# A recommender tower kernel: first-layer chunks spread over four tiles, and known parts of the MLP moved into the last quad

## The chip, the core and the metric

The kernel runs on one core of a Trainium2 chip. The metric is the device time of one execution, in microseconds (us). It is launched once, with all inputs in device memory.

## What is computed

The reference looks up 39 embedding rows of 16 floats for each of 512 samples, runs three layers of a compressed interaction network over them, and feeds the summed layers and a dense context to a small MLP. Everything is float32.

```python
def cin_layer(X0, Xi, W, b):                   # W: (128, 39 * Fi)
    return einsum('hjk,bjd,bkd->bhd', W.reshape(128, 39, Fi), X0, Xi) + b
e = stack([tbl_f[ids[:, f]] for f in range(39)], axis=1)     # 512 x 39 x 16
X1 = cin_layer(e, e, W0, b0); X2 = cin_layer(e, X1, W1, b1); X3 = cin_layer(e, X2, W2, b2)
z = concat([X1.sum(2), X2.sum(2), X3.sum(2), dense_ctx])     # 128 + 128 + 128 + 16
h = relu(z @ W_top1 + b_top1)                                # 400 -> 512
h = relu(h @ W_top2 + b_top2)                                # 512 -> 256
y = h @ W_top3                                               # 256 -> 1
```

## The kernel before, in words

**Tiles and quads.** A tile T is 8 samples times 16 dimensions = 128 columns; there are 64. Four tiles are a quad q (512 columns); there are 16. `ti` is a tile's place in its quad, 0 to 3. In the last quad there is no next quad to prepare.

**Layer 1, the main loop.** `layer1(T, g)` (L645) multiplies a tile of X1 with W1 in ten groups g of up to four fields, by three matmuls of 512 columns (L657 to L659: high and low parts). Their results go round a ring of five PSUM banks, `ps_y`, so group g needs the bank that group g-5 has left (for g below 5: group g+5 of the tile before). Seven groups (0, 1, 3, 4, 6, 7, 9) are scaled by ACT (`scale`, L415), three (2, 5, 8) by DVE (`scale_and_sum`, L527 and L529), into `prod`. POOL adds two pairs of ACT's groups (`add_groups`, L323): the first when ACT has done group 1, the second when ACT has done group 4. DVE reduces the early half (`reduce_early`, L536) after POOL's second add, then scales group 8, then reduces the late half (`reduce_late`, L544). ACT may begin the next tile only when the early half is reduced. `sum_d` (L665) multiplies the reduced tile with a block pattern, and ACT keeps the result (`keep_g`, L424).

**Layer 0, one quad ahead.** While quad q runs its tiles, X1 of quad q+1 is made. SP copies three blocks of rows (`share_rows`, L237, three DMAs) and cuts six windows (`cut_window`, L242, six DMAs) as soon as the rows are there. POOL multiplies each of seven chunks c = 0 to 6 with the shared rows (`multiply`, L318) and signals `z_made`. TensorE then runs `layer0(q+1, c)` (L600), one fp32 matmul, which shows as two instructions, into the bank `ps_x1`.

**The order of the work** is written out by hand. POOL runs, for each tile, the first add, `between(q, ti, 0)`, the second add, `between(q, ti, 1)`. `MULTIPLIED_IN` (L66) says in which of these places chunks are multiplied, and `GATHERED_IN` (L67) where the table rows of quad q+3 are gathered (L298, ten per quad). `SUMMED_AFTER` (L69) says after which (ti, group) TensorE runs each layer-0 chunk. TensorE executes its list in order and waits where an operand is not ready.

**The end.** After the last tile TensorE makes the MLP's first layer in four banks of `ps_y` from four inputs: the dense context (16 rows) and X1's sums `r1` (both known early), X2's sums (after the last `sum_d`) and X3's sums `r3`. `r3` comes from 39 fp32 matmuls (L703, 78 instructions) over all samples. Then come the second layer (L713) and the third (L718). The bias is added to `r1` by DVE after the last tile (L570).

Of the kernel before, what the change touches and what calls it, by code (L numbers as in the profile page):

```python
# [5 lines left out]
ALU = mybir.AluOpType  # L6
ACT = mybir.ActivationFunctionType
# [18 lines left out]
SPC = 3  # L26
CHUNKS = -(-SHIFTS // SPC)
REP = SPC * F
MOVES = SPC + CHUNKS - 1
XROWS = REP + CHUNKS - 1  # L30
FPG = P // QB
GATHERS = -(-F // FPG)
# [30 lines left out]
REDUCTIONS = 2  # L63


MULTIPLIED_IN = {(1, 0): range(0, 1), (1, 1): range(1, 4), (2, 0): range(4, 5), (2, 1): range(5, CHUNKS)}  # L66
GATHERED_IN = {(0, 0): range(0, 1), (0, 1): range(1, 5), (3, 0): range(5, 6), (3, 1): range(6, GATHERS)}  # L67
REPEATED_IN = (2, 1)
SUMMED_AFTER = {(1, 8): 0, (2, 0): 1, (2, 2): 2, (2, 4): 3, (2, 6): 4, (2, 9): 5, (3, 1): 6}  # L69
SUM_D_AFTER = 6  # L70


HALF = FIRST[GROUPS // 2] * H
# [36 lines left out]
def build(nc, dense_ctx, ids, bases, table, W_top1, b_top1, W_top2, b_top2, W_top3, W0, b0, W1, b1, W2, b2, out):  # L110
# [8 lines left out]
    with ExitStack() as ctx:  # L119
# [3 lines left out]
        def sem(name):  # L123
            return ctx.enter_context(nc.semaphore(name))
# [73 lines left out]
        shifted = [sem("shifted_0"), sem("shifted_1")]  # L198
# [19 lines left out]
        def _(sp):  # L218
# [46 lines left out]
            sp.dma_start(dense_t_dram, dense_out).then_inc(w2_saved, 16)  # L265
            for q in range(1, QUADS):
                sp.wait_ge(x0_made, q + 1)
                share_rows(q, shifted[q % 2])
                for c in range(1, CHUNKS):
                    cut_window(q, c, shifted[q % 2])  # L270
                if q + 1 < QUADS:
                    lay_out(q + 1)

# [15 lines left out]
        def _(pool):  # L289
# [20 lines left out]

            def multiply(q, c):
                if c == 0:
                    wait(pool, shifted[q % 2], 16 * MOVES * ((q + 1) // 2))
                r = chunk_rows(c)
                window = bz[0:r, c, :] if c else x0[0:r, q % 2, :]
                if c == 0:
                    wait(pool, z_used, CHUNKS * (q - 1) + 1)
# [40 lines left out]
        def _(act):  # L358
# [94 lines left out]
            nc.scalar.copy(y_row[0:1, :], ps_tr[0:1, :]).then_inc(y_out, 1)  # L453

        @block.vector
        def _(dve):
# [94 lines left out]
            for T in range(TILES):  # L551
                q, ti = T // QT, T % QT
                if ti == 0:
                    dve.wait_ge(xt_made, q + 1)
                if T > 0:
                    reduce_late(T - 1)
                scale_and_sum(T, DVE_GROUPS[0])
                scale_and_sum(T, DVE_GROUPS[1])
                if ti == 3 and q + 1 < QUADS:
                    split_x1(q + 1)  # L560
                reduce_early(T)
                scale_and_sum(T, DVE_GROUPS[2])
                if ti == 3 and q + 1 < QUADS:
                    sum_x1(q + 1)
                if ti == 1 and q + 1 < QUADS:
                    spread(q + 1)
            reduce_late(TILES - 1)
            dve.wait_ge(bsum_made, 1)
            dve.wait_ge(r1_made, QUADS)
            nc.vector.tensor_scalar(r1[:], r1[:], b02_sum[:, 0:1], None, ALU.add).then_inc(r1_done, 1)  # L570

        @block.tensor
        def _(pe):
# [71 lines left out]
            def layer1(T, g):  # L645
# [12 lines left out]
                nc.tensor.matmul(y, hi, w1_lo[:, cols], start=False, stop=False)  # L658
                nc.tensor.matmul(y, lo, w1_hi[:, cols], start=False, stop=True).then_inc(y_made, 1)  # L659

            def sum_d(T):
                pe.wait_ge(reduced, REDUCTIONS * (T + 1))
                pe.wait_ge(bd_made, T // QT + 1)
                wait(pe, g_kept, T)
                nc.tensor.matmul(ps_g[:, 0:(F + 1) * TB], x2[:, T % 2, :],  # L665
                                 bd[:, T // QT % 2, T % QT].rearrange("p j b -> p (j b)"),
                                 start=True, stop=True).then_inc(g_summed, 1)

            for T in range(TILES):
# [4 lines left out]
                for g in range(GROUPS):  # L674
# [10 lines left out]
            def mlp1(c, rows_c, z, start, stop):  # L685
                for m in range(MC1):
                    ins = nc.tensor.matmul(ps_y[:, m, :], wt1[0:rows_c, c, m * P:(m + 1) * P], z,  # L687
                                           start=start, stop=stop)
                    if stop:
                        ins.then_inc(h1_summed, 1)  # L690
# [17 lines left out]
            for m in range(MC2):  # L708
                dst = ps_y[:, YBANKS - 1, :] if m == 0 else ps_g[:]
                for c in range(MC1):  # L710
                    if m == 0:
                        pe.wait_ge(h1_made, c + 1)
                    ins = nc.tensor.matmul(dst, wt2[:, c, m * P:(m + 1) * P], h1[:, c, :],  # L713
                                           start=c == 0, stop=c == MC1 - 1)
                ins.then_inc(h2_summed, 1)
# [39 lines left out]
```

## Time and profile before

| | before |
|---|---|
| median of three runs | 722.71 us (721.22 to 723.44) |
| the profiled execution | 718.87 us |
| its span, first to last instruction | 717.1 us |
| TensorE busy | 671.6 us, 94% |
| ScalarE (ACT) busy | 541.1 us, 75% |
| VectorE (DVE) busy | 469.7 us, 66% |
| GpSimd (POOL) busy | 460.5 us, 64% |
| mean granted TensorE clock | 0.983 of full speed |

Times in a timeline are a start and a length in us from the span's first instruction, then engine, line, operation, output and inputs, and in brackets the idle time of that engine just before it with what released it. Matmul ends are modelled, so two matmuls in a row overlap on paper. The reliable number is the distance from start to start. A table of stretches gives, for each stretch, its length, the busy time (and number of instructions) of PE, PEld (weight load), DVE, ACT and POOL, the granted clock, the busy share of the DMA engines, and GB/s.

### The profile page before, as it was taken

Reading aid. Unit: us, or ns where it says so; the run is one execution under the profiler, and the core shown is the slowest. Engines: PE = TensorE matmul, PEld = TensorE weight load, DVE = VectorE, ACT = ScalarE, POOL = GpSimd, SP = SyncE. Lnnn points to the kernel's source line nnn. Section 1 sums busy time; section 2 is a strip of 40 time slices with the busy share of each in tenths; the row PEclk is TensorE's granted clock in tenths of the full one; section 3 lists DMA queues with packets and bytes.
Section 4 is the critical chain, followed back from the end, with each engine's and each line's share of the span. In section 5 each row is a group of like instructions: output and inputs, shape, how many; then the busy total and the mean of one; then the engine's idle time right before and its main releaser. Section 6 shows DMA issues by size and latency. Waiting matters only on the chain. (4 is left out here: it accounts for less than half of the span.)

```text
span 717.1 us, 10090 instructions
## 1 busy us (share of the span) xinstructions
PE 671.6 (94%) x2631; PEld 481.9 (67%) x2631; DVE 469.7 (66%) x954; ACT 541.1 (75%) x1939; POOL 460.5 (64%) x445
## 2 busy tenths in 40 slices
PE   4597999999999999999999999999999999998998
PEld 4464777777677767676767677776777776774443
DVE  6245677778677777777676777786777777784000
ACT  4255797979797979888897979797979798993003
POOL 6765686877778686868686868777785736321000
PEclk9699999999999999999999999999999999998999
DMA  6664040404031312213040404040313122300000
GB/s 202 220 176 97 1 99 1 98 1 98 2 95 6 92 8 73 26 41 59 16 84 3 98 2 97 2 97 3 96 4 93 5 79 91 143 1 0 0 1 0
DMA packets 103772, 41.40 MB, mean 58 GB/s; under 512 B 86961, under 2 KB 90033, under 8 KB 103074
## 3 DMA queue, kind: packets, MB, share of 16 engines
q1 hardware_dynamic: 98594, 39.47, 21.7%
q0 software_dynamic: 5120, 1.29, 2.2%
q8 instruction: 21, 0.34, 0.2%
q14 instruction: 37, 0.30, 0.1%
HBM read 11.29 MB, written 2.59 MB: 19 GB/s over the span
## 5 line engine op out<-in xcount | busy, mean ns | idle before, releaser
L415 ACT ACTIVATE prod<-ps_y,xt 128x128 f32<-128x128 f32 x1792 | 498.1, 452 | 88.0 <-PE ps_y L659 79.4
L657 PE MATMUL ps_y<-w_hi,x_hi 128*128 128x512 f32 (+1 forms) x640 | 307.9, 481 | 16.2 <-DVE prod L529 14.4
L323 POOL TENSOR_TENSOR prod<-prod 128x512 f32<-128x512 f32 x128 | 165.6, 1294 | 133.6 <-ACT prod L415 132.0
L659 PE MATMUL ps_y<-w_hi,x_lo 128*128 128x512 f32 (+1 forms) x640 | 249.2, 389 | 0.0
L658 PE MATMUL ps_y<-w_lo,x_hi 128*128 128x512 f32 (+1 forms) x640 | 248.9, 389 | 0.0
L529 DVE SCALAR_TENSOR_TENSOR prod<-ps_y,xt,prod 128x128 f32<-128x128 f32 x576 | 163.8, 343 | 48.0 <-PE ps_y L659 46.2
L298 POOL DMA_INDIRECT rows<-in_table,index x160 | 153.4, 959 | 42.7 <-issue 35.7
L657 PEld LDWEIGHTS ps_y<-w_hi,x_hi 128*128 128x128 f32 x640 | 120.8, 189 | 72.3 <-DVE prod L529 26.3
L536 DVE TENSOR_REDUCE prod<-prod 128x128 f32<-128x1536 f32 x64 | 112.2, 1753 | 85.3 <-ACT prod L415 53.0
L658 PEld LDWEIGHTS ps_y<-w_lo,x_hi 128*128 128x128 f32 x640 | 120.8, 189 | 47.1 <-issue 25.5
L659 PEld LDWEIGHTS ps_y<-w_hi,x_lo 128*128 128x128 f32 x640 | 120.5, 188 | 25.3
L318 POOL TENSOR_TENSOR room<-room 117x512 f32<-117x512 f32 (+1 forms) x105 | 133.4, 1288 | 5.5 <-DMA room<-room 5.5
L544 DVE TENSOR_REDUCE x<-prod 128x128 f32<-128x1536 f32 x64 | 111.9, 1748 | 15.8 <-ACT prod L415 14.1
L600 PE MATMUL ps_x<-room,w0t 117*128 117x512 f32 (+1 forms) x224 | 114.5, 596 | 5.0 <-POOL room L318 5.0
L600 PEld LDWEIGHTS ps_x<-room,w0t 117*128 117x128 f32 (+1 forms) x224 | 42.1, 190 | 17.4 <-issue 7.9
L527 DVE TENSOR_SCALAR prod<-ps_y,xt 128x128 f32<-128x128 f32 x128 | 38.6, 343 | 11.4 <-PE ps_y L659 11.4
L665 PE MATMUL ps_g<-bd,x 128*128 128x320 f32 x128 | 44.8, 431 | 0.0
L424 ACT COPY g_all<-ps_g 128x320 f32<-128x320 f32 x64 | 33.3, 520 | 11.9 <-PE ps_g L665 11.9
L703 PE MATMUL ps_x<-g_all,room 128*128 128x512 f32 x78 | 33.6, 592 | 0.0
L444 ACT ACTIVATE w0t<-ps_x,columns 128x512 f32<-128x512 f32 x1 | 0.7, 688 | 37.4 <-PE ps_x L703 37.4
L665 PEld LDWEIGHTS ps_g<-bd,x 128*128 128x128 f32 x128 | 24.0, 188 | 6.1 <-issue 0.5
L703 PEld LDWEIGHTS ps_x<-g_all,room 128*128 128x128 f32 x78 | 14.8, 190 | 18.7 <-issue 18.7
(62 smaller groups left out, 235.9 us busy)
## 6 DMA issues: line engine op xcount, KB each, us to landing
room<-room SPq DMA_DIRECT2D x80, 234.0 KB
room<-room SPq DMA_DIRECT2D x48, 78.0 KB
emb_room<-rows SPq DMA_DIRECT2D x180, 5.0 KB
rows<-in_table,index POOLq DMA_INDIRECT x160
g_all<-in_L_rec_W SPq DMA_DIRECT2D x1, 2496.0 KB, 9.8
room<-room SPq DMA_DIRECT2D x16, 156.0 KB
w2t_dram<-g_all SPq DMA_DIRECT2D x1, 2496.0 KB
room<-w2t_dram SPq DMA_DIRECT2D x1, 2496.0 KB, 8.9
```

The source lines that it names most:

```text
L298: pool.indirect_dma_start(out=rows[0:n, q % 2, g, :], out_offset=None, in_=table, in_offset=bass.IndirectOffsetOnAxis(ap=index[0:n, q % 2, ...
L318: nc.gpsimd.tensor_tensor(bz[0:r, c, :], window, xa[0:r, :], ALU.mult).then_inc(z_made, 1)
L323: nc.gpsimd.tensor_tensor(prod[:, SLOT[a]:SLOT[a] + 2], prod[:, SLOT[a]:SLOT[a] + 2], prod[:, SLOT[b]:SLOT[b] + 2], ALU.add).then_inc(pool ...
L415: ins = nc.scalar.activation(prod[:, SLOT[k] + m // 2, :, m % 2], ps_y[:, g % YBANKS, m * H:(m + 1) * H], ACT.Copy, scale=xt[:, q % 2, ti, ...
L529: ins = nc.vector.scalar_tensor_tensor(out=a, in0=y, scalar=x, in1=a, op0=ALU.mult, op1=ALU.add)
L536: nc.vector.tensor_reduce(prod[:, BIASED, :, 0], prod[:, EARLY].rearrange("p n h l -> p h n l"), AX_XY, ALU.add).then_inc(reduced, 1)
L544: nc.vector.tensor_reduce(x2[:, T % 2, :], prod[:, LATE[T % 2]].rearrange("p n h l -> p h n l"), AX_XY, ALU.add).then_inc(reduced, 1)
L600: nc.tensor.matmul(ps_x1[:], w0t[0:r, c, :], bz[0:r, c, :], start=c == 0, stop=c == CHUNKS - 1).then_inc(z_used, 1)
L657: nc.tensor.matmul(y, hi, w1_hi[:, cols], start=True, stop=False)
L658: nc.tensor.matmul(y, hi, w1_lo[:, cols], start=False, stop=False)
L659: nc.tensor.matmul(y, lo, w1_hi[:, cols], start=False, stop=True).then_inc(y_made, 1)
L665: nc.tensor.matmul(ps_g[:, 0:(F + 1) * TB], x2[:, T % 2, :], bd[:, T // QT % 2, T % QT].rearrange("p j b -> p (j b)"), start=True, stop=Tr ...
```

## The change

1. The seven layer-0 chunks of the next quad ran one in tile 1, five in tile 2 and one in tile 3. They now run one, two, two, two in tiles 0 to 3, each after another group.
2. POOL's multiplies move with them: chunks 0 and 1 to tile 0, after its second add; chunk 2 and chunk 3 to tile 1; the rest stays. Chunk 0 now waits only for the three shared rows, chunk 1 for the six windows, where before chunk 0 waited for all nine DMAs. The gathers that stood in that place move to tiles 1 and 2.
3. In the last quad, after group 3 of each tile, TensorE runs one fp32 matmul of the MLP's first layer: the dense and the `r1` part of output chunks 0 and 1, into the idle banks of `ps_tr` and `ps_x1`. Parts for chunks 2 and 3 follow right after the last tile, into ring banks as they come free. The bias of `r1` is added in the last quad's first tile.
4. At the end `r3` is made first and the part from X2's sums behind it. The last layer-0-free banks are dealt out anew, and the second layer runs inputs 0 to 2 for both outputs before input 3.

```diff
-MULTIPLIED_IN = {(1, 0): range(0, 1), (1, 1): range(1, 4), (2, 0): range(4, 5), (2, 1): range(5, CHUNKS)}
-GATHERED_IN = {(0, 0): range(0, 1), (0, 1): range(1, 5), (3, 0): range(5, 6), (3, 1): range(6, GATHERS)}
+MULTIPLIED_IN = {(0, 1): range(0, 2), (1, 0): range(2, 3), (1, 1): range(3, 4), (2, 0): range(4, 5),
+                 (2, 1): range(5, CHUNKS)}
+GATHERED_IN = {(0, 0): range(0, 1), (0, 1): range(1, 2), (1, 1): range(2, 4), (2, 1): range(4, 5),
+               (3, 0): range(5, 6), (3, 1): range(6, GATHERS)}
-SUMMED_AFTER = {(1, 8): 0, (2, 0): 1, (2, 2): 2, (2, 4): 3, (2, 6): 4, (2, 9): 5, (3, 1): 6}
+SUMMED_AFTER = {(0, 9): 0, (1, 4): 1, (1, 9): 2, (2, 3): 3, (2, 8): 4, (3, 0): 5, (3, 2): 6}
+MLP_AFTER = {(0, 3): (0, 0), (1, 3): (1, 0), (2, 3): (0, 1), (3, 3): (1, 1)}
+        ps_h1 = [ps_tr[:], ps_x1[:], ps_y[:, 0, :], ps_y[:, 1, :]]
+        ps_r3 = ps_y[:, 2, :]
+        ps_h2 = [ps_y[:, 3, :], ps_y[:, 4, :]]
+        ps_out = ps_g[0:1, :]
...
             def multiply(q, c):
                 if c == 0:
-                    wait(pool, shifted[q % 2], 16 * MOVES * ((q + 1) // 2))
+                    wait(pool, shared[q % 2], 16 * SPC * ((q + 1) // 2))
+                    wait(pool, z_used, CHUNKS * (q - 1) + 1)
+                if c == 1:
+                    wait(pool, cut[q % 2], 16 * (CHUNKS - 1) * ((q + 1) // 2))
...
+                if T == TILES - QT:
+                    dve.wait_ge(bsum_made, 1)
+                    dve.wait_ge(r1_made, QUADS)
+                    nc.vector.tensor_scalar(r1[:], r1[:], b02_sum[:, 0:1], None, ALU.add).then_inc(r1_done, 1)
             reduce_late(TILES - 1)
-            dve.wait_ge(bsum_made, 1)
-            dve.wait_ge(r1_made, QUADS)
-            nc.vector.tensor_scalar(r1[:], r1[:], b02_sum[:, 0:1], None, ALU.add).then_inc(r1_done, 1)
...
+            def known_mlp1(m, part):
+                if (m, part) == (0, 0):
+                    pe.wait_ge(late_mlp, 64)
+                    pe.wait_ge(bd_made, QUADS)
+                    pe.wait_ge(x1_lo_made, QUADS)
+                    pe.wait_ge(r1_made, QUADS)
+                if (m, part) == (0, 1):
+                    pe.wait_ge(r1_done, 1)
+                w, z = (wt1[0:C, 3, m * P:(m + 1) * P], dense_t[:]) if part == 0 else (wt1[:, 0, m * P:(m + 1) * P], r1[:])
+                nc.tensor.matmul(ps_h1[m], w, z, start=part == 0, stop=False)
...
+                    if not nxt and (ti, g) in MLP_AFTER:
+                        known_mlp1(*MLP_AFTER[ti, g])
...
-            pe.wait_ge(late_mlp, 64)
-            pe.wait_ge(act_step, ACT_STEPS * TILES)
-            pe.wait_ge(dve_step, DVE_STEPS * TILES)
-            mlp1(3, C, dense_t[:], True, False)
-            pe.wait_ge(r1_done, 1)
-            mlp1(0, P, r1[:], False, False)
+            for m in range(2, MC1):
+                if m == 2:
+                    pe.wait_ge(dve_step, DVE_STEPS * (TILES - 1) + DVE_DONE[YBANKS])
+                else:
+                    pe.wait_ge(act_step, ACT_STEPS * (TILES - 1) + ACT_GROUPS.index(YBANKS + 1) + 1)
+                for part in range(2):
+                    known_mlp1(m, part)
             sum_d(TILES - 1)
             pe.wait_ge(late_w2, 16)
             pe.wait_ge(g_kept, TILES)
-            mlp1(1, P, g_all[:, F, :], False, False)
+            pe.wait_ge(act_step, ACT_STEPS * TILES)
             for j in range(F):
-                ins = nc.tensor.matmul(ps_x1[:], w2t[:, j * H:(j + 1) * H], g_all[:, j, :],
-                                       start=j == 0, stop=j == F - 1)
+                ins = nc.tensor.matmul(ps_r3, w2t[:, j * H:(j + 1) * H], g_all[:, j, :], start=j == 0, stop=j == F - 1)
             ins.then_inc(r3_summed, 1)
+            for m in range(MC1):
+                nc.tensor.matmul(ps_h1[m], wt1[:, 1, m * P:(m + 1) * P], g_all[:, F, :], start=False, stop=False)
             pe.wait_ge(r3_made, 1)
-            mlp1(2, P, r3, False, True)
+            for m in range(MC1):
+                nc.tensor.matmul(ps_h1[m], wt1[:, 2, m * P:(m + 1) * P], r3, start=False,
+                                 stop=True).then_inc(h1_summed, 1)
```

## Rows read from the trace of the kernel before

**Rows 1.** The page, busy time of each engine.

```profile
PE 671.6 (94%) x2631; PEld 481.9 (67%) x2631; DVE 469.7 (66%) x954; ACT 541.1 (75%) x1939; POOL 460.5 (64%) x445
```

**Rows 2.** Table of stretches: quads 5, 13 and 0.

```profile
241.10:279.16 38.06, 36.95 (x152) 27.54 (x150) 28.21 (x56) 32.71 (x120) 29.27 (x29) 1.00 0.23 47
545.88:583.25 37.37, 36.96 (x151) 27.55 (x150) 28.21 (x56) 32.59 (x120) 22.53 (x21) 1.00 0.22 47
44.70:88.91 44.21, 39.14 (x153) 28.82 (x154) 25.03 (x52) 31.06 (x113) 26.83 (x27) 0.96 0.34 99
```

**Rows 3.** Table of stretches: tiles 0 and 1 of quad 5.

```profile
241.10:248.45 7.35, 7.35 (x34) 5.98 (x33) 6.02 (x14) 7.35 (x30) 6.04 (x8) 1.00 0.56 168
248.45:258.59 10.14, 9.03 (x40) 6.52 (x38) 7.14 (x14) 9.02 (x34) 9.05 (x9) 1.00 0.43 52
```

**Rows 4.** Timeline of TensorE, tile 1 of quad 5, group 3.

```profile
251.82 0.50 PE L657 MATMUL ps_y<-w_hi,x_hi 128*128 128x512 f32 x1 [1.11 <-DVE prod L529]
```

**Rows 5.** Timeline of TensorE, a layer-0 chunk before group 9, tile 1.

```profile
257.04 1.02 PE L600 MATMUL ps_x<-room,w0t 117*128 117x512 f32 x2
257.50 0.79 PE L657 MATMUL ps_y<-w_hi,x_hi 128*128 128x512 f32 x1
258.13 0.39 PE L658 MATMUL ps_y<-w_lo,x_hi 128*128 128x512 f32 x1
```

**Rows 6.** Timeline of POOL, tiles 0 and 1 of quad 5.

```profile
246.85 0.97 POOL L298 DMA_INDIRECT rows<-in_table,index  x1 [0.28 <-POOL index L292]
247.84 1.31 POOL L323 TENSOR_TENSOR prod<-prod 128x512 f32<-128x512 f32 x1
...
254.02 1.32 POOL L323 TENSOR_TENSOR prod<-prod 128x512 f32<-128x512 f32 x1
255.28 1.29 POOL L318 TENSOR_TENSOR room<-room 117x512 f32<-117x512 f32 x1
```

**Rows 7.** Timeline of TensorE, first group of tile 1, quad 5.

```profile
248.45 0.40 PE L657 MATMUL ps_y<-w_hi,x_hi 128*128 128x512 f32 x1
```

**Rows 8.** Timelines of SP, POOL and TensorE in quad 0.

```profile
54.90 4.80 SPq L242 DMA_DIRECT2D room<-room  x6
...
63.77 1.26 POOL L318 TENSOR_TENSOR room<-room 117x512 f32<-117x512 f32 x1 [5.49 <-DMA room<-room]
...
65.17 2.05 PE L600 MATMUL ps_x<-room,w0t 117*128 117x512 f32 x2 [5.03 <-POOL room L318]
```

**Rows 9.** Timelines of POOL and TensorE, quad 13, tiles 0 and 1.

```profile
551.95 1.29 POOL L323 TENSOR_TENSOR prod<-prod 128x512 f32<-128x512 f32 x1 [0.77 <-ACT prod L415]
...
553.25 0.40 PE L657 MATMUL ps_y<-w_hi,x_hi 128*128 128x512 f32 x1
...
555.91 0.50 PE L657 MATMUL ps_y<-w_hi,x_hi 128*128 128x512 f32 x1 [0.41 <-DVE prod L529]
```

**Rows 10.** Table of stretches: two at a low clock.

```profile
64.90:68.30 3.40, 3.13 (x6) 1.83 (x6) 1.96 (x3) 0.00 (x0) 3.40 (x4) 0.50 0.23 8
...
655.40:662.20 6.80, 6.80 (x9) 2.49 (x8) 0.00 (x0) 0.00 (x0) 0.00 (x0) 0.50 0.00 0
```

**Rows 11.** Table of stretches: the last quad's first and last tile.

```profile
619.86:627.75 7.89, 7.63 (x33) 5.86 (x32) 7.17 (x15) 7.89 (x32) 2.59 (x2) 1.00 0.23 99
...
642.89:650.46 7.57, 7.57 (x33) 5.71 (x31) 6.35 (x14) 7.57 (x30) 2.59 (x2) 1.00 0.00 1
```

**Rows 12.** Chain that ended last, in order of time.

```profile
652.75 10.64 PE ps_y L687 x16
...
664.53 3.67 PE ps_y L687 x8
668.21 33.49 PE ps_x L703 x78
...
702.52 3.70 PE ps_y L687 x8
```

**Rows 13.** Timeline of DVE, the last late reduction.

```profile
652.69 1.75 DVE L544 TENSOR_REDUCE x<-prod 128x128 f32<-128x1536 f32 x1
```

More of the change, by code:

```diff
@@ L28 @@
 REP = SPC * F
-MOVES = SPC + CHUNKS - 1
 XROWS = REP + CHUNKS - 1
@@ L197, in build @@
         emb_turned, x0_made = sem("emb_turned"), sem("x0_made")
-        shifted = [sem("shifted_0"), sem("shifted_1")]
+        shared = [sem("shared_0"), sem("shared_1")]
+        cut = [sem("cut_0"), sem("cut_1")]
         first_shared = sem("first_shared")
@@ L267, in _ @@
                 sp.wait_ge(x0_made, q + 1)
-                share_rows(q, shifted[q % 2])
+                share_rows(q, shared[q % 2])
                 for c in range(1, CHUNKS):
-                    cut_window(q, c, shifted[q % 2])
+                    cut_window(q, c, cut[q % 2])
                 if q + 1 < QUADS:
@@ L312, in multiply @@
                 if c == 0:
-                    wait(pool, shifted[q % 2], 16 * MOVES * ((q + 1) // 2))
+                    wait(pool, shared[q % 2], 16 * SPC * ((q + 1) // 2))
+                    wait(pool, z_used, CHUNKS * (q - 1) + 1)
+                if c == 1:
+                    wait(pool, cut[q % 2], 16 * (CHUNKS - 1) * ((q + 1) // 2))
                 r = chunk_rows(c)
                 window = bz[0:r, c, :] if c else x0[0:r, q % 2, :]
-                if c == 0:
-                    wait(pool, z_used, CHUNKS * (q - 1) + 1)
                 nc.gpsimd.tensor_tensor(bz[0:r, c, :], window, xa[0:r, :], ALU.mult).then_inc(z_made, 1)
@@ L443, in _ @@
             act.wait_ge(r3_summed, 1)
-            nc.scalar.activation(r3, ps_x1[:], ACT.Identity, bias=b02_sum[:, 1:2]).then_inc(r3_made, 1)
+            nc.scalar.activation(r3, ps_r3, ACT.Identity, bias=b02_sum[:, 1:2]).then_inc(r3_made, 1)
             for m in range(MC1):
                 act.wait_ge(h1_summed, m + 1)
-                nc.scalar.activation(h1[:, m, :], ps_y[:, m, :], ACT.Relu, bias=bt1[:, m:m + 1]).then_inc(h1_made, 1)
+                nc.scalar.activation(h1[:, m, :], ps_h1[m], ACT.Relu, bias=bt1[:, m:m + 1]).then_inc(h1_made, 1)
             for m in range(MC2):
                 act.wait_ge(h2_summed, m + 1)
-                src = ps_y[:, YBANKS - 1, :] if m == 0 else ps_g[:]
-                nc.scalar.activation(h2[:, m, :], src, ACT.Relu, bias=bt2[:, m:m + 1]).then_inc(h2_made, 1)
+                nc.scalar.activation(h2[:, m, :], ps_h2[m], ACT.Relu, bias=bt2[:, m:m + 1]).then_inc(h2_made, 1)
             act.wait_ge(y_summed, 1)
-            nc.scalar.copy(y_row[0:1, :], ps_tr[0:1, :]).then_inc(y_out, 1)
+            nc.scalar.copy(y_row[0:1, :], ps_out).then_inc(y_out, 1)
         @block.vector
@@ L683, in _ @@
                         layer0(q + 1, SUMMED_AFTER[ti, g])
[L685 to L690, printed above, removed]
-            pe.wait_ge(late_mlp, 64)
-            pe.wait_ge(act_step, ACT_STEPS * TILES)
-            pe.wait_ge(dve_step, DVE_STEPS * TILES)
-            mlp1(3, C, dense_t[:], True, False)
-            pe.wait_ge(r1_done, 1)
-            mlp1(0, P, r1[:], False, False)
+                    if not nxt and (ti, g) in MLP_AFTER:
[7 more added lines that the diff above has]
+                    known_mlp1(m, part)
             sum_d(TILES - 1)
@@ L700, in _ @@
             pe.wait_ge(g_kept, TILES)
-            mlp1(1, P, g_all[:, F, :], False, False)
+            pe.wait_ge(act_step, ACT_STEPS * TILES)
             for j in range(F):
-                ins = nc.tensor.matmul(ps_x1[:], w2t[:, j * H:(j + 1) * H], g_all[:, j, :],
-                                       start=j == 0, stop=j == F - 1)
+                ins = nc.tensor.matmul(ps_r3, w2t[:, j * H:(j + 1) * H], g_all[:, j, :], start=j == 0, stop=j == F - 1)
             ins.then_inc(r3_summed, 1)
+            for m in range(MC1):
+                nc.tensor.matmul(ps_h1[m], wt1[:, 1, m * P:(m + 1) * P], g_all[:, F, :], start=False, stop=False)
             pe.wait_ge(r3_made, 1)
-            mlp1(2, P, r3, False, True)
[L708 to L715, printed above, removed]
+            for m in range(MC1):
+                nc.tensor.matmul(ps_h1[m], wt1[:, 2, m * P:(m + 1) * P], r3, start=False,
+                                 stop=True).then_inc(h1_summed, 1)
+            for half in (range(MC1 - 1), range(MC1 - 1, MC1)):
+                for m in range(MC2):
+                    for c in half:
+                        if m == 0:
+                            pe.wait_ge(h1_made, c + 1)
+                        ins = nc.tensor.matmul(ps_h2[m], wt2[:, c, m * P:(m + 1) * P], h1[:, c, :],
+                                               start=c == 0, stop=c == MC1 - 1)
+                    if MC1 - 1 in half:
+                        ins.then_inc(h2_summed, 1)
             for m in range(MC2):
                 pe.wait_ge(h2_made, m + 1)
-                ins = nc.tensor.matmul(ps_tr[0:1, :], wt3[:, m:m + 1], h2[:, m, :], start=m == 0, stop=m == MC2 - 1)
+                ins = nc.tensor.matmul(ps_out, wt3[:, m:m + 1], h2[:, m, :], start=m == 0, stop=m == MC2 - 1)
             ins.then_inc(y_summed, 1)
```

## The prediction

> **What bounds the kernel now.** I read the page first: TensorE is busy 94% of the span, the others 75% or less [rows 1], so a change pays by TensorE's own work or its gaps. Then the table of stretches, one for each quad. A middle quad takes 38.06 us, of which TensorE works 36.95; quads 1 to 12 all look like this. Quad 13, where POOL gathers nothing more, takes 37.37 with the same 36.96 of work [rows 2]. So each quad holds one gap. The table by tile finds it: tile 0 runs without a gap in 7.35 us (its bare work: ten groups and one `sum_d`), tile 1 takes 10.14 and works 9.03 [rows 3].
>
> The timeline names the gap. Tile 1 begins at 248.45 [rows 7] and its group 3 at 251.82 [rows 4]. Three groups at 0.70 each (nine of them, the short group 8 and `sum_d` make the 7.35 of tile 0) would put it at 250.55, so 1.27 us are lost, and the row says that it waited for DVE. DVE was late with group 8 of tile 0, since that comes behind `reduce_early`, and that waits for POOL's second add, at 247.84 to 249.15, which stood behind a gather [rows 6]. In quad 13 the gap is 555.91 - 553.25 - 2.10 = 0.56 us [rows 9].
>
> **Part 1, chunks spread over four tiles.** Neither matmuls nor multiplies become more. A chunk costs TensorE 0.86 us: it starts at 257.04 and the second matmul of the group behind it at 258.13, less that group's 0.23 between matmuls [rows 5]. All seven run wherever they stand, so if every tile is bound by TensorE, spreading them moves work and saves none. What can be saved is the gap (1.27 us twelve times, 0.56 twice) by filling it. In exchange there may be a wait for a chunk that isn't ready.
>
> That wait decides the case. Chunk 0 now stands behind group 9 of tile 0, where TensorE arrives at 248.45 [rows 7]. Its product is made by POOL behind the second add of the same tile. That add starts at 247.84; a multiply starts 1.26 after an add and lasts 1.29 (254.02, 255.28) [rows 6]; TensorE starts 0.14 after its end (63.77 + 1.26 = 65.03, then 65.17) [rows 8]. So 247.84 + 1.26 + 1.29 + 0.14 = 250.53: TensorE waits **2.08 us**, with all of tile 1 queued behind the chunk. The index and the gather before the add stay where they were, so nothing brings it forward. Nor is it chance: group 9 needs the bank that ACT's group 4 leaves, and POOL's add waits for the same group 4, so TensorE has one group (0.70) to run while POOL has an add and a multiply. With no gather in the way, in quads 13 and 14, it is 551.95 + 2.69 - 553.25 = 1.39 us [rows 9].
>
> Does the old gap stay beside it? Tile 1 would begin 2.08 + 0.86 late, at 251.4, and reach group 3 at 253.5; DVE frees that bank at about 251.8 [rows 4], so it is gone. The exchange is 2.08 for 1.27 in twelve quads and 1.39 for 0.56 in two: +0.81 and +0.83 by starts. The restart after the old gap costs another 0.11 (0.34 instead of 0.23 between its first matmuls), which the restart on a chunk may or may not cost. That makes 0.70 to 0.82; I take 0.75. 14 x 0.75 = **+10.5 us**.
>
> What else moves: POOL's tile 0 loses three gathers (0.97 and 0.28 of idle each [rows 6], 3.8 us) and gets two multiplies (2.6). Chunk 1 waits for the windows. In quad 0 these landed 4.07 us after their last issue (54.90 + 4.80 = 59.70, multiply at 63.77) [rows 8]. SP issues them in quad 5 until 247.9, so by 252.0 at the latest; chunk 1 is then ready at 253.3 and is wanted, behind group 4 of tile 1, at about 255.4. POOL's first add of tile 1 is behind one more gather, at 254.5, when ACT has group 1. In tile 2 POOL has two adds, three multiplies, the row repeat and one gather, 2.6 + 3.9 + 0.6 + 1.25 = 8.3 us in a tile of 9.5. The other chunks are ready 1.5 us or more before their places. I count these at nothing; if the cover goes, 0.3 to 0.6 us a quad.
>
> In quad 0, TensorE now waits for the shared rows in tile 0, where before it waited 5.03 us in tile 1. They land between 54.9 (issued) and 58.9 (the same 4.07 later) [rows 8]; with twice as little queued ahead of them as of the windows I take 58. Chunk 0 is ready at 59.4, and 36.7 - 7.35 = 29.4 of work remain (36.7 is the quad of 38.06 without its gap and restart), to 88.8. The idle time has brought the clock down once before, to 1.2 GHz from 64.90 to 68.30 [rows 10], which costs half the stretch; I take 1.2, and 0.4 of small waits: 90.4 against 88.91 [rows 2]. **+1.4 us** (0 to 2.5).
>
> **Part 2, the MLP's parts in the last quad.** Each is one fp32 matmul, two instructions at 33.49 / 78 = 0.43 us, 0.86 together [rows 12]. The first tile takes 7.89, the others 7.57 [rows 11] against 7.35 of bare work, so only 0.22 a tile is free. First tile 7.89 + 0.86, as its gap lies at group 3, ahead of the new matmul; the other three 7.35 + 0.86 = 8.21. Together 33.4 against 30.6: +2.8.
>
> Behind the last tile (call its end X, 650.46 before) TensorE waited 2.3 us, ran 16 instructions in 10.64, of which 6.80 us at half clock, and reached `r3` at 668.21, X + 17.75 [rows 10, 12]. Now eight instructions (3.43) run at once. Then `sum_d` waits for the last late reduction, which before ended at X + 3.98 [rows 13]; with ACT less behind TensorE I take 3.7 (3.43 to 3.98). `sum_d` and the copy behind it take 664.53 - 663.39 = 1.14, with 0.1 to start: `r3` begins at X + 4.9. From there: 33.5 for `r3`, 3.4 for the X2 part, which now stands here and covers ACT's pass over `r3`, so the 0.82 from 701.70 to 702.52 goes; then 14.5 as before: 51.4. The last quad and the end take 33.4 + 4.9 + 51.4 = 89.7 against 97.2 (619.86 to 717.06): **-7.5 us**. The end of the second layer is not shorter: the last two instructions of each output still stand last. The bias of `r1` costs DVE 0.48 in a tile where it isn't last.
>
> By the Trainium skill (SBUF, on the shared port pair) VectorE in a two-port mode locks GpSimd out for a whole instruction; the `r1` bias could then hold one of POOL's adds for 0.48 us. The multiplies all lasted 1.26 to 1.31 us beside VectorE here, so no row shows such a lock; with it the sum would be at most 0.5 higher.
>
> **Sum.** 10.5 + 1.4 - 7.5 = +4.4. On the profiled execution 718.87 + 4.4 = 723.3. The median of the runs is 3.84 above that execution; I carry the difference over: 722.71 + 4.4 = **727.1 us**.
>
> **The rivals.**
> - *A, POOL is earlier.* If the second add of tile 0 comes as in quad 13, the wait is 1.39 everywhere and the twelve quads cost about +0.1 each: 1.2 + 1.5 + 1.4 - 7.5 = -3.4, 719.3. For: gather and add have free room before them. Against: the diff leaves that gather in place. The balance turns where the wait falls below 2.08 - 4.4 / 14 = 1.77 us. This is the case on the other side.
> - *B, no wait at all*, the change does what spreading suggests: 12 x 1.38 + 2 x 0.67 = 17.9 and 7.5 saved, 697. Against it stands the order of POOL's list.
> - *C, the clock falls after each new wait.* The wait of 5.03 us was followed by 3.4 us at half clock [rows 8, 10], the gaps of 1.27 by none; 2.08 lies between. 14 x 1.7 = 24 more: 751. The Trainium skill (TensorE: Matmul & The Clock Gate, Part 1) says that activity releases the throttle and idleness brings it back; it would allow this case.
> - *D, the clock still falls at the end*, as two of the four instruction pairs there have 16 rows as before: 3.4 of the 7.5 stay, 730.5.
> - *E, new waits in tiles 1 and 2*, where POOL has more: 0.4 x 14, 732.7.
>
> **Chances.** Forecast 0.60, A 0.12, B 0.04, C 0.05, D 0.12, E 0.07. A measurement of this kernel can tell about 0.3%, 2.2 us, from no change. The forecast's own range is 724 to 730 (0.1 a quad, 1.5 in quad 0, 1 at the end); a fifth of it lies within 2.2 us of no change. Slower 0.48 + D, C, E 0.24 = 0.72, same 0.12, faster 0.16. The range 718.5 to 731 holds the forecast, A and D.
>
> **What would show it.** Right: in a middle quad of the new trace TensorE's idle time lies ahead of a chunk (the layer-0 line), released by POOL's multiply, about 2.1 us long, 1.4 in quads 13 and 14; the quad lasts 38.8; group 3 of tile 1 has no gap; the last quad's later tiles take 8.2, no low clock stands behind 655, and `r3` begins 5 us behind the last group. Wrong: quads under 38.3, a multiply of chunk 0 that starts more than 0.7 us earlier in its quad, or a low clock in the middle.

## The result and the profile after

| | before | after |
|---|---|---|
| median of the runs | 722.08 us (721.22 to 723.44) | 738.8 us (736.92 to 740.4) |
| ratio | | 1.0234 (95%: 1.0211 to 1.0257) |
| the profiled execution, its span | 718.87, 717.1 us | 736.92, 735.1 us |
| mean granted TensorE clock | 0.983 | 0.970 |
| first group of tile 0 / of tile 60 / end | 44.7 / 619.9 / 717.1 | 45.4 / 644.0 / 735.1 |

The kernel is 2.3% slower, where 727.1 us had been forecast (slower by 0.6%). The direction was right, the size was not: 738.8 lies above the range. The page after has the busy times nearly unchanged; TensorE's rises by ten microseconds, though it does the same work in the loop.

```profile
PE 681.9 (93%) x2631; PEld 491.1 (67%) x2631; DVE 470.6 (64%) x954; ACT 545.5 (74%) x1939; POOL 463.0 (63%) x445
```

The table of stretches, taken for single quads (length, busy time of PE, PEld, DVE, ACT, POOL, granted clock, DMA share, GB/s), shows why. These are quads 1, 4, 5, 13 and 0 of the changed kernel; they answer to [rows 2].

```profile
91.38:130.20 38.82, 36.95 (x152) 27.55 (x150) 28.26 (x56) 32.76 (x120) 29.36 (x29) 1.00 0.23 46
209.39:249.74 40.35, 38.49 (x151) 28.70 (x150) 28.24 (x56) 32.97 (x120) 29.38 (x29) 0.96 0.21 45
249.74:288.56 38.82, 36.95 (x152) 27.56 (x151) 28.25 (x56) 32.76 (x120) 29.38 (x29) 1.00 0.22 46
568.45:606.62 38.17, 36.96 (x151) 27.55 (x150) 28.26 (x56) 32.76 (x120) 22.52 (x21) 1.00 0.22 46
45.35:91.38 46.03, 40.40 (x152) 29.98 (x153) 24.99 (x52) 31.49 (x113) 26.98 (x27) 0.93 0.33 95
```

There are two kinds of middle quad. Quads 1 and 5 take 38.82 us at full clock, what the prediction worked out to a tenth. Quad 4 takes 40.35 at a mean clock of 0.96, and its TensorE is "busy" 1.54 us longer for the same instructions. In this execution five of quads 1 to 12 are of the first kind and seven (3, 4, 6, 7, 9, 10, 12) of the second. The other three executions took 738.4 to 740.4 us at a mean clock of 0.963 to 0.965, so they had more half clock than this one. The timeline of TensorE at the end of tile 0 looks the same in both; first quad 5, then quad 6:

```profile
259.12 1.10 PE L612 MATMUL ps_x<-room,w0t 117*128 117x512 f32 x2 [1.87 <-POOL room L330]
259.65 0.79 PE L669 MATMUL ps_y<-w_hi,x_hi 128*128 128x512 f32 x1
...
297.93 1.27 PE L612 MATMUL ps_x<-room,w0t 117*128 117x512 f32 x2 [1.87 <-POOL room L330]
298.46 1.16 PE L669 MATMUL ps_y<-w_hi,x_hi 128*128 128x512 f32 x1
299.42 0.63 PE L670 MATMUL ps_y<-w_lo,x_hi 128*128 128x512 f32 x1
299.85 0.63 PE L671 MATMUL ps_y<-w_hi,x_lo 128*128 128x512 f32 x1
```

In both, chunk 0 waited for POOL's multiply. The 1.87 is the gap that is left when the modelled length of the matmul before is taken off. From start to start chunk 0 comes 2.26 us behind that matmul, and 0.23 of it is the matmul itself, so the wait is 2.0 us; the waits below are counted in this way. In quad 6 the matmuls behind it stand 0.43 us apart instead of 0.23. The stretch behind the wait ran at half clock:

```profile
298.70:302.10 3.40, 3.40 (x9) 2.43 (x8) 2.23 (x3) 1.39 (x5) 2.27 (x2) 0.50 0.27 11
```

The 18.0 us by which the two spans differ add up: the first tile begins 0.65 later; quad 0 +1.8; twelve quads with the longer wait, 12 x 0.76 = +9.1; seven of them at a low clock, 7 x 1.56 = +10.9; quads 13 and 14 +1.6; last quad and end -6.1 (91.1 instead of 97.2).

### The profile page after: what moved, and what is told of

The parts are those of the page before. It is cut to its first block and busy times, and to the rows that moved or that the text cites. A ratio compares the mean times of both kernels' runs of the same rounds, so it can differ in the third digit from the quotient of the medians.

```text
span 735.1 us, 10091 instructions
## 1 busy us (share of the span) xinstructions
PE 681.9 (93%) x2631; PEld 491.1 (67%) x2631; DVE 470.6 (64%) x954; ACT 545.5 (74%) x1939; POOL 463.0 (63%) x445
## 5 line engine op out<-in xcount | busy, mean ns | idle before, releaser
L669 PE MATMUL ps_y<-w_hi,x_hi 128*128 128x512 f32 (+1 forms) x640 | 315.1, 492 | 2.0 <-DVE x_lo L496 1.7
L670 PE MATMUL ps_y<-w_lo,x_hi 128*128 128x512 f32 (+1 forms) x640 | 253.5, 396 | 0.0
L671 PE MATMUL ps_y<-w_hi,x_lo 128*128 128x512 f32 (+1 forms) x640 | 253.1, 396 | 0.0
L669 PEld LDWEIGHTS ps_y<-w_hi,x_hi 128*128 128x128 f32 x640 | 123.6, 193 | 54.8 <-issue 21.7
L670 PEld LDWEIGHTS ps_y<-w_lo,x_hi 128*128 128x128 f32 x640 | 123.9, 194 | 51.0 <-issue 26.7
L612 PE MATMUL ps_x<-room,w0t 117*128 117x512 f32 (+1 forms) x224 | 118.6, 615 | 30.6 <-POOL room L330 30.6
L538 DVE TENSOR_SCALAR prod<-ps_y,xt 128x128 f32<-128x128 f32 x128 | 38.8, 345 | 22.1 <-PE ps_y L671 21.4
L724 PE MATMUL ps_y<-g_all,room 128*128 128x512 f32 x78 | 33.7, 593 | 0.6 <-issue 0.6
L724 PEld LDWEIGHTS ps_y<-g_all,room 128*128 128x128 f32 x78 | 14.7, 190 | 19.2 <-issue 19.2
L489 DVE TENSOR_TENSOR bd<-ps_tr,mask 128x1248 f32<-128x1248 f32 x16 | 23.2, 1449 | 5.3 <-ACT xt L382 5.3
```

What stands on the lines that cost most here:

```text
L612: nc.tensor.matmul(ps_x1[:], w0t[0:r, c, :], bz[0:r, c, :], start=c == 0, stop=c == CHUNKS - 1).then_inc(z_used, 1)
L669: nc.tensor.matmul(y, hi, w1_hi[:, cols], start=True, stop=False)
L724: ins = nc.tensor.matmul(ps_r3, w2t[:, j * H:(j + 1) * H], g_all[:, j, :], start=j == 0, stop=j == F - 1)
```

## The experiments

The theory after the result: the wait for chunk 0 costs its own length, and beyond that brings TensorE's clock down behind it in some quads. The rivals: the low clock comes from the new mix of matmuls; or the loss lies in the MLP part.

The runs were made on several chips, and these are of two kinds. On one the first tile begins at 45 us and the kernel before takes 722 to 723 us; on the other it begins at 63 to 69 and the kernel before takes 743 to 745. So each run has a ratio to the kernel before on its own chip, and beside it I give the time from the first group of tile 0 to the end, which leaves out what comes ahead of the first tile: 672.4 us for the kernel before (traced on the first kind of chip alone), 689.8 for the changed one. Quad 0 can still differ between the two kinds by 3 us. Each count of quads is taken from one profiled execution.

**Each part alone.** The chunk schedule in the kernel before, and the MLP part with the old tables:

```diff
 # e1_chunks_only: the kernel before, plus
+MULTIPLIED_IN, GATHERED_IN, SUMMED_AFTER and the split waits of multiply() as in the change
 # e2_mlp_only: the changed kernel, but
+MULTIPLIED_IN, GATHERED_IN, SUMMED_AFTER as before the change
```

> The kernel before with part 1 alone: the new places of the chunks, their multiplies and the gathers, and the split waits on the DMAs. Last quad and end as before. Theory: all of the loss lies here, 24.2 us up to the start of the last quad in the trace of the changed kernel, so this kernel takes about 722 + 23 = 745 us, with low-clock stretches in some of the middle quads right behind the wait for chunk 0. Rival (the loss comes from the MLP parts in the last quad or at the end): 722 to 730.

> The changed kernel with the chunks, multiplies and gathers put back to the places of before: part 2 alone. Theory: the last quad and the end take 91.1 us instead of 97.2, so 722 - 6 = 716 us, middle quads 38.05. Rival (part 2 gains nothing by itself): 720 to 724.

Part 1 alone: ratio 1.0302 (1.0224 to 1.0379), 699.7 us from the first tile to the end, low clock in eight of the twelve middle quads, last quad and end 98.9, with 10.2 us at half clock instead of 6.8. Part 2 alone: ratio 0.9854 (0.9792 to 0.9917), 663.4 us, middle quads 38.04 to 38.09 (one, quad 9, 38.33), last quad and end 91.1. The whole loss is part 1's, and part 2 by itself gains 6.1 us in the last quad and the end. The other 2.9 of the 9.0 us between 672.4 and 663.4 stand in quad 0 (41.3 against 44.2), which has the order of the kernel before. SP had issued the copies for quad 1 before the first tile there, and behind it in the trace of the kernel before, so these are not the change's. Two quads of part 1 alone (one of each kind), and a quad of part 2 alone:

```profile
193.83:234.26 40.43, 38.55 (x152) 28.56 (x151) 28.39 (x56) 33.10 (x120) 29.51 (x29) 0.96 0.22 45
274.62:313.45 38.83, 36.95 (x152) 27.56 (x150) 28.36 (x56) 32.76 (x120) 29.42 (x29) 1.00 0.22 46
```

```profile
260.31:298.35 38.04, 36.95 (x152) 27.51 (x151) 28.31 (x56) 32.72 (x120) 29.31 (x29) 1.00 0.23 47
```

**The wait filled with useless work**, so that its length stays and its idleness goes:

```diff
                 if c == 0:
                     wait(pe, x1_lo_made, q)
                     wait(pe, r1_made, q)
+                    for _ in range(8 if q else 0):
+                        nc.tensor.matmul(ps_x1[:], x1_hi[:, (q - 1) % 2, 0:P], w1_hi[:, 0:512], start=True, stop=True)
```

> The changed kernel with eight extra matmuls (8 x 0.23 = 1.9 us) ahead of chunk 0 of each next quad, on the operands of group 0, into the bank that chunk 0 clears: TensorE works where it waited. The product is ready no earlier. Theory (the idle wait brings the clock down): quads of 38.8 us throughout, no low clock in the middle, 738.8 - 11 to 13 = 726 to 728 us. Rival 1 (the low clock has another cause, the mix of matmuls in tile 1): quads of 40.4 remain, 737 to 740. Rival 2 (the extra matmuls themselves lengthen the way to chunk 0): quads over 39.

```profile
114.83:153.63 38.80, 38.80 (x159) 29.05 (x158) 28.34 (x56) 32.77 (x120) 29.45 (x29) 1.00 0.23 46
270.04:308.84 38.80, 38.80 (x159) 29.05 (x158) 28.34 (x56) 32.77 (x120) 29.45 (x29) 1.00 0.22 46
541.98:580.82 38.84, 38.84 (x159) 29.05 (x158) 28.34 (x56) 32.88 (x120) 29.45 (x29) 1.00 0.22 46
```

Eight instructions more a quad, and 9.7 us less in all (680.1): eleven of the twelve quads take 38.8, one 39.05, none is at a low clock. Chunk 0 comes no sooner and, but for the eight in the wait, the matmuls around it are the same, so in the middle quads it is the idleness that costs the clock. The ratio to the kernel before is 1.007 (1.0036 to 1.0105): about the size I had forecast (1.006), though from the first tile to the end it is 7.7 us above the kernel before, where the forecast's sum has 4.4.

**The wait made shorter and longer.** One gather moved from ahead of the second add to behind it, and a second one put ahead of it:

```diff
 # e5_gather_later
-GATHERED_IN = {(0, 0): range(0, 1), (0, 1): range(1, 2), (1, 1): range(2, 4), ...
+GATHERED_IN = {(0, 1): range(0, 2), (1, 1): range(2, 4), ...
 # e11_longer_wait
-GATHERED_IN = {(0, 0): range(0, 1), (0, 1): range(1, 2), (1, 1): range(2, 4), ...
+GATHERED_IN = {(0, 0): range(0, 2), (1, 1): range(2, 4), ...
```

> The changed kernel with the one gather that stood between the two adds of tile 0 moved behind them. Chunk 0's multiply then starts 0.7 us earlier. Theory: TensorE waits 1.39 us instead of 2.08 at the end of tile 0, tile 0 lasts 9.25 instead of 9.90, and as in quads 13 and 14 (which have that wait already) the clock does not fall: all middle quads 38.15, none of 40.4; from the first tile to the end 17 to 20 us less than the changed kernel's 689.8. Rival (any wait of TensorE of more than 1.3 us can bring the clock down): tile 0 at 9.25, but quads of 39.7 among them.

> The changed kernel with a second gather ahead of the second add of tile 0: chunk 0's product comes 1.25 us later, the wait of TensorE is 3.33 us instead of 2.08. Theory (the longer the wait, the surer the low clock behind it: in none of 14 quads at 1.39, in 7 of 12 at 2.08): tile 0 lasts 11.1, the low clock follows in all twelve quads 1 to 12, which then take 38.8 + 1.25 + 1.6 = 41.6 us. Rival (the clock falls by a pattern that has nothing to do with the length): again about half of the quads, the others at 40.1.

| wait for chunk 0 | quads 1 to 12 with a low clock | length without it | first tile to end |
|---|---|---|---|
| 1.4 us (e5; 1.5 in quad 8) | 0 of 12 | 38.2 | 674.6 |
| 2.0 us, 2.3 in quad 9 (after; e1; e7, below) | 7; 8; 9 of 12 | 38.8 | 689.8; 699.7; 691.6 |
| 2.0 us, filled (e3) | 0 of 12 | 38.8 | 680.1 |
| 3.2 us, 3.5 in quad 9 (e11) | 12 of 12 | none | 718.4 |

Ratios: 0.9991 (0.9964 to 1.0018) with the shorter wait, 1.0583 (1.0546 to 1.062) with the longer. Two of the quads with the longer wait; the second is one of four in which the low clock lasted 6.8 us:

```profile
91.91:133.54 41.63, 38.55 (x152) 28.58 (x150) 28.26 (x56) 32.89 (x120) 29.26 (x29) 0.96 0.21 43
175.17:218.04 42.87, 39.78 (x152) 29.34 (x150) 28.32 (x56) 32.89 (x120) 29.38 (x29) 0.92 0.20 42
```

The wait itself, as TensorE's timeline of that kernel has it in quad 5:

```profile
270.24 1.97 PE L612 MATMUL ps_x<-room,w0t 117*128 117x512 f32 x2 [3.08 <-POOL room L330]
```

With the shorter wait the quads are 38.2 in all, 0.15 more than before the change: the exchange of one gap for another, without the clock. From the first tile to the end it gained 15 us where 17 to 20 had been expected, as quad 0 took 48.0 and the last quad and end 92.4, with 3.4 us of half clock. The longer the wait, the surer the low clock; what decides which of the quads with 2.0 us have it, the runs don't show. The Trainium skill (TensorE: Matmul & The Clock Gate, Part 1) says that the clock is throttled by default and released by activity. The fill agrees: with matmuls in the wait none of the twelve quads had a low clock.

**Chunk 0 multiplied sooner.**

```diff
 # e4_swap
-MULTIPLIED_IN = {(0, 1): range(0, 2), (1, 0): range(2, 3), ...
+MULTIPLIED_IN = {(0, 0): range(0, 1), (0, 1): range(1, 2), (1, 0): range(2, 3), ...
-GATHERED_IN = {(0, 0): range(0, 1), (0, 1): range(1, 2), ...
+GATHERED_IN = {(0, 1): range(0, 2), ...
 # e8_swap_and_later: as e4, and chunk 1 to tile 1
+MULTIPLIED_IN = {(0, 0): range(0, 1), (1, 0): range(1, 2), (1, 1): range(2, 4), ...
+SUMMED_AFTER = {(0, 9): 0, (1, 6): 1, (1, 9): 2, ...
```

> The changed kernel with chunk 0's multiply and the first gather of tile 0 swapped: POOL multiplies chunk 0 before its second add and gathers after it. The order and number of all else stays. Theory: the product is there 0.4 us before TensorE comes to it, no wait at the end of tile 0, no low clock; what is left is 0.4 us of the old gap at group 3 of tile 1, so middle quads of 37.1 and 722 - 14 x 0.9 + 2 - 6 = 705 us. Rival (the multiply only pushes the second add and with it the early reduction; the old gap comes back): quads of 38.0, 718 us.

> As the kernel with chunk 0's multiply and the first gather swapped, where POOL waited 2.4 us for the windows in tile 0 and the quads came out at 37.1 to 38.1; here chunk 1's multiply moves to tile 1 (POOL: chunk 1 between the adds, chunks 2 and 3 behind them) and TensorE runs chunk 1 behind group 6. Theory: no wait on a DMA, no wait at the end of tile 0, middle quads 37.1 and from the first tile to the end 655. Rival (three multiplies in tile 1 push the adds and the gap comes back a tile later): 37.5 to 38.

Neither has a low clock in quads 1 to 14. Ratios 0.983 (0.9768 to 0.9892) and 0.9814 (0.9757 to 0.9871), 664.3 and 660.2 us. The quads of the first, 37.3 to 38.1, missed the 37.1 expected. Its POOL timeline shows what I had priced at nothing, chunk 1's wait for the windows:

```profile
272.16 1.29 POOL L330 TENSOR_TENSOR room<-room 117x512 f32<-117x512 f32 x1 [2.35 <-DMA room<-room]
273.61 1.00 POOL L309 DMA_INDIRECT rows<-in_table,index  x1 [0.16 <-issue]
274.91 0.94 POOL L309 DMA_INDIRECT rows<-in_table,index  x1 [0.30 <-issue]
275.86 1.30 POOL L335 TENSOR_TENSOR prod<-prod 128x512 f32<-128x512 f32 x1
```

The add of tile 1 at 275.86 is late behind the wait and two gathers. With chunk 1 in tile 1 the quads come to 37.4 to 37.7.

**Chunk 0 run later**, behind group 2 of tile 1, ahead of the group that has the old gap; and the same with the gather later.

```diff
 # e6_chunk0_in_tile1
-SUMMED_AFTER = {(0, 9): 0, (1, 4): 1, ...
+SUMMED_AFTER = {(1, 2): 0, (1, 4): 1, ...
 # e12_tile1_gather_later: as e6, and GATHERED_IN of e5
```

> The changed kernel with one entry moved: TensorE runs chunk 0 behind group 2 of tile 1 instead of behind group 9 of tile 0. POOL's list is untouched. Theory: the product is ready when TensorE gets there, so there is no wait at the end of tile 0, and the chunk fills most of the old gap at group 3; middle quads 37.1 to 37.3, no low clock, from the first tile to the end about 655 us against 689.8 of the changed kernel and 672.4 of the kernel before. Rival (group 3 still waits as long as before, the chunk comes on top): quads of 38.0.

> The changed kernel with chunk 0 behind group 2 of tile 1 and the first gather of tile 0 behind the second add, nothing else: how much of the combined kernel is due to the gather. Theory: the old gap at group 3 shrinks by the 0.7 us that POOL's second add comes earlier, middle quads 36.7 to 36.8 as in quad 13 of the kernel with chunk 0 moved alone (36.73), against 37.21 there. Rival (POOL is then late in tile 1): 37.2 or more.

One entry of a table turns the change round: ratio 0.9811 (0.9759 to 0.9863), 660.1 us, ten of the quads 1 to 12 at 37.2, no low clock there. The 655 expected was missed outside them: quad 0 took 47.7, and the last quad and end 92.6, with 3.4 us at half clock. The gather that was to bring 0.5 us more a quad brought nothing: 37.2 to 38.3, 665.2 us, ratio 0.985 (0.9809 to 0.9892). Its POOL timeline shows the same cause as above; my expectation had read quad 13, where the gathers aren't moved but absent:

```profile
252.13 1.29 POOL L330 TENSOR_TENSOR room<-room 117x512 f32<-117x512 f32 x1
255.06 1.30 POOL L330 TENSOR_TENSOR room<-room 117x512 f32<-117x512 f32 x1 [1.63 <-DMA room<-room]
256.52 1.00 POOL L309 DMA_INDIRECT rows<-in_table,index  x1 [0.16 <-issue]
257.82 0.95 POOL L309 DMA_INDIRECT rows<-in_table,index  x1 [0.30 <-issue]
258.79 1.29 POOL L335 TENSOR_TENSOR prod<-prod 128x512 f32<-128x512 f32 x1
```

**The 16-row parts of the MLP.** In the changed kernel a dense part takes longer than the 0.86 us of the sum. The timeline of TensorE in tile 60:

```profile
647.10 0.39 PE L671 MATMUL ps_y<-w_hi,x_lo 128*128 128x512 f32 x1
647.42 1.12 PE L683 MATMUL ps_tr<-dense_t,emb_room 16*128 16x512 f32 x2
648.47 0.50 PE L669 MATMUL ps_y<-w_hi,x_hi 128*128 128x512 f32 x1
648.80 0.40 PE L670 MATMUL ps_y<-w_lo,x_hi 128*128 128x512 f32 x1
```

From the matmul before to the one behind it is 1.37 us, where an `r1` part of 128 rows would make it 0.23 + 0.86 = 1.09. The next one comes 0.33 later instead of 0.23, which makes 0.38 in all. The timeline of the weight loads (PEld) has both loads start together with their matmuls:

```profile
647.42 0.29 PEld L683 LDWEIGHTS ps_tr<-dense_t,emb_room 16*128 16x128 f32 x2 [0.36 <-issue]
648.47 0.19 PEld L669 LDWEIGHTS ps_y<-w_hi,x_hi 128*128 128x128 f32 x1 [0.76 <-ACT prod L427]
```

```diff
 # e7_full_rows, which leaves the dense context out of the result (one execution)
-                w, z = (wt1[0:C, 3, m * P:(m + 1) * P], dense_t[:]) if part == 0 else (wt1[:, 0, m * P:(m + 1) * P], r1[:])
+                w = wt1[:, 0, m * P:(m + 1) * P]
+                z = wt2[:, 0:2, :].rearrange("p c m -> p (c m)") if part == 0 else r1[:]
```

> The changed kernel in which the MLP's dense part (16 rows) is replaced by a product of two loaded operands of 128 rows and the same 512 columns; the dense context is left out of the result. In the changed kernel such a part takes 1.05 us in the chain of the last quad, where a 128-row part takes 0.86, and 1.24 from the group before to the group behind. Theory: the weights of a matmul with another number of rows are not loaded beside the matmul before, which costs about 0.2 us at each change of the row count: here group 3 of tile 60 to group 4 is 0.4 shorter, the eight instructions behind the last tile take 3.4 instead of 4.2, and the last quad with the end 91.07 - 1.5 = 89.6. Rival (the extra lies in opening a new bank): no difference, 91.1.

```profile
702.50 3.43 PE ps_y L684 x8
```

The chain of waits has the eight instructions behind the last tile in 3.43 us here; the changed kernel has them in 4.21:

```profile
678.36 4.21 PE ps_y L683 x8
```

Last quad and end take 89.65, as expected to 0.1. It is the number of rows, not the opening of a bank. And the weights do load earlier here: the part's at 672.08, ahead of its matmul at 672.23, and group 4's at 672.66, together with the second instruction of the part. The next kernel, e10, has the same four 16-row instructions side by side behind its last tile, so the number of rows changes twice there and not four times. From the first of the eight instructions to `sum_d` it takes 3.73 us (649.94 to 653.67) against 4.12 in the changed kernel (678.28 to 682.40). So the 0.2 us go with the change and not with the small number of rows.

**What the experiments point to**, in two versions. The first has `FIRST_QUAD`, the old tables for quad 0, and puts the 16-row parts side by side; the second puts two things right that the first one's trace showed.

```diff
 # e10_combined, against the changed kernel
+SUMMED_AFTER = {(1, 2): 0, (1, 4): 1, (1, 9): 2, (2, 3): 3, (2, 8): 4, (3, 0): 5, (3, 2): 6}
+GATHERED_IN = {(0, 1): range(0, 2), (1, 1): range(2, 4), (2, 1): range(4, 5), ...
+MLP_AFTER = {(0, 3): [(0, 0), (1, 0)], (2, 3): [(0, 1)], (3, 3): [(1, 1)]}
+quad 0 with MULTIPLIED_IN, GATHERED_IN and SUMMED_AFTER of the kernel before
 # e13_chunk1_later, against e10
+MULTIPLIED_IN = {(0, 1): range(0, 1), (1, 0): range(1, 2), (1, 1): range(2, 4), (2, 0): range(4, 5), ...
+SUMMED_AFTER = {(1, 2): 0, (1, 6): 1, (1, 9): 2, ...
+MLP_AFTER as in the changed kernel
```

> What the experiments point to: chunk 0 behind group 2 of tile 1, the first gather of tile 0 behind the second add, the first quad in the order of the kernel before (where the rows land late), the 16-row parts of the MLP side by side (two behind group 3 of the last quad's first tile, two behind the last tile). Theory: middle quads 36.75, quad 0 about 44, last quad with the end 90.3, from the first tile to the end 648 us against 672.4 of the kernel before and 689.8 of the changed one: 24 us, 3.3%, under the kernel before. Rival (the later gathers push POOL's adds in tile 1): middle quads of 37.2 to 37.6, 655 us.

> As the combined kernel, with two things put right that its trace showed. First, POOL multiplied chunk 1 in tile 0, waited 1.6 us for the windows there and took the gathers and the adds of tile 1 late (tile 2 then 9.8 to 10.4 instead of 9.44); here chunk 1 is multiplied between the adds of tile 1 and run behind group 6. Second, its two 16-row parts side by side were followed by a low clock; here each stands alone again, as in the changed kernel. Theory: middle quads 36.75, quad 0 about 45, last quad with the end 91.1, from the first tile to the end 649 to 650 us against 672.4 of the kernel before and 661.0 of the combined one, a ratio to the kernel before of about 0.968. Rival (the old gap at group 3 has another cause than POOL's lateness): tile 2 stays over 9.8, middle quads 37.3 and more, 656 us.

The first: ratio 0.9749 (0.972 to 0.9778), 661.0 us instead of 648, quads of 37.1 to 38.2. And its last quad begins with a tile of 11.49 us, in which half clock followed the two 16-row parts, though TensorE's one gap there was of 0.25 us, at 616.7:

```profile
614.20:625.69 11.49, 11.24 (x38) 7.60 (x36) 7.88 (x15) 8.28 (x32) 2.56 (x2) 0.85 0.21 90
619.40:622.80 3.40, 3.40 (x9) 2.57 (x9) 0.83 (x5) 1.15 (x4) 0.39 (x2) 0.50 0.00 0
```

This was the slowest of its six executions (708.2, the others 702.5 to 706.0) and had the lowest granted clock (0.981, the others 0.985 to 0.988), so the half clock need not be in all of them.

The second: ratio **0.9652 (0.9626 to 0.9677)**, 647.0 us from the first tile to the end, 25.4 less than the kernel before. (Of these, 2.6 stand in quad 0, which took 41.6 instead of 44.2 with the same order: on this chip the copies for quad 1 had been issued before it began. Without them the time is in the 649 to 650 expected.) A middle quad, and the last quad with the end:

```profile
257.22:293.97 36.75, 36.75 (x151) 27.56 (x150) 28.25 (x56) 32.71 (x120) 29.37 (x29) 1.00 0.23 49
...
624.45:715.51 91.06, 88.08 (x261) 47.37 (x259) 30.77 (x59) 39.41 (x133) 10.36 (x8) 1.00 0.03 13
```

The middle quads are 36.75 to 36.85, with hardly a gap on TensorE: the bare work of 36.7 that the prediction had taken from the old trace. POOL's lateness in tile 1 had been the cause of the rest, as the two kernels have the same order in these quads but for the places of chunks 1 and 2.

## Why the prediction was right and wrong

- **What bounds the kernel, and the old gap**: right. Part 2 alone keeps quads of 38.05; the last version, which fills the gap, is 1.3 us a quad shorter and TensorE has none left.
- **The wait for chunk 0, 2.08 us**: right, it was 2.03. Chunk 0 came at 259.12, 9.38 us behind the quad's start at 249.74; the forecast was 250.53 - 241.10 = 9.43. The 38.8 of a quad stood in the prediction, and quads 1, 2, 5, 8 and 11 have it. Quads 13 and 14 wait 1.37 for the 1.39 forecast and take 0.80 more than before.
- **The exchange at 0.75 a quad**: it was 0.76 in quads 1 to 12 and 0.80 in the other two: 10.7 instead of 10.5 us.
- **The clock**: this step failed. The sum put the low clock behind the new waits at nothing, and the range left it out; it stood as rival C at a chance of 0.05 and all or nothing, 24 us. The trace put 10.9 us there, seven quads at 1.56 where I had 14 at 1.7, and the fill (none of 12) shows that the wait's idleness brings it. What I had before me were a wait of 5.03 us with a low clock behind it and gaps of 1.27 without one [rows 4, 8, 10]; 2.08 lies between, nearer to the harmless one, and I gave the price of the harmless end. Not allowed for was a mixture: the same wait is followed by a low clock in some quads and not in others of one execution. With a wait of unknown effect between two measured ones, half the price should have gone into the sum, or at least into the range. That half would have come near the seven of fourteen is hindsight. The measured +18.0 us is 13.6 above the sum's +4.4: this step is 10.9 of them, the end 1.4, and the later first tile, quad 0 and the exchange 1.3 together.
- **Quad 0, +1.4** (90.4 less 88.91 is 1.5): it was +1.8. Chunk 0 started at 60.07 where I had 59.4 and a start 0.65 earlier. The low clock behind the wait came as forecast.
- **The last quad, +2.8**: four tiles took 34.2 instead of 30.6, so +3.6. The price of 0.86 for each part was the term mis-sized: it is 1.24 for one of 16 rows (tile 60 takes 9.11, and 8.74 with 128 rows in e7). The two tiles with an `r1` part take 8.23, as forecast. The same 0.8 us lies in the parts behind the last tile.
- **The end, -7.5 in all**: -6.1, by that same term. `r3` began 5.5 us behind the last group where I had 4.9. That no low clock would stand there held in this execution, but not without luck: e5 and e6 run the same instructions there and had 3.4 us at half clock (92.4 and 92.6 for last quad and end), which is rival D.
- **POOL's moves, counted at nothing**: right for the changed kernel, where TensorE came 2 us late anyway and hid it; its POOL waited 1.0 us for the windows. In the kernels without the wait it was worth up to 0.9 us in tile 2 alone (10.38 in e12 against 9.44). The cover was the wait itself. By the working's own numbers chunk 1 was wanted at 254.9 and not 255.4 (251.4 and five groups of 0.70); nothing hung on it.
- **Rival A** (ratio 0.995 forecast, 719.3): e5 is that kernel and came at 0.9991. Its quads were 38.2 against my 38.05 + 0.1, its last quad and end 92.4, with the low clock just named.
- **The lock of POOL by DVE's bias**: no POOL add in tile 60 is longer than 1.3 us.

## What to carry to other kernels

Where a producer and the in-order engine that needs it are released by the same event, count from that event along both lists before moving a consumer forward: here one group of TensorE's work stood against an add and a multiply. Price a new wait on TensorE at its own length and, once it is longer than the gaps that the trace shows to be harmless, at a stretch of half clock behind it in part of the cases. Spreading work evenly over stages saves nothing by itself; the 36.75 us quad came from putting each chunk behind its product and POOL's DMA wait behind its urgent adds.

## What the runs showed of the hardware

- TensorE's clock fell at idle waits of about 2.0 us (2.3 in one quad of each run) in 7, 8 and 9 of 12 cases, of 3.2 us in 12 of 12, of 1.4 us in none of 12, and with the 2.0 us filled by matmuls in none. A stretch of 3.4 us at 1.2 GHz behind a 2.0 us wait cost 1.56 us.
- Idleness is not the only thing behind which it fell. In e5 and e6 TensorE ran the last tile and the eight MLP instructions behind it with no gap, and 3.4 us of half clock began at 683.4 and at 673.6, with the last of the eight; the changed kernel and seven other runs have the same instructions there and no low clock. In e10 two adjacent fp32 matmuls of 16 rows (from 617.6 on) were followed by half clock from 619.4 to 622.8, but the two behind its last tile (from 649.9 on) were not. In the kernel before, half clock from 655.40 followed 16-row matmuls too, but TensorE had waited 2.3 us just ahead of these [rows 10, 12]. So that a small number of rows has a part in it is a guess that no run isolates.
- A matmul with another number of rows than the one before it costs about 0.2 us: eight instructions in 4.21 us with four changes of row count, 3.43 with none, and 0.39 less from the first to `sum_d` with two changes than with four. The traces have its weights loaded together with it, where those of a matmul with the same number of rows are loaded beside the matmul before.
